# A one-core language-model tower: another order of TensorE's work ahead of the scan, dt products over all 128 rows, and the first dt*u products made inside the softplus

## What is computed

```python
xi, z = jnp.split(layernorm(x, gamma_in, beta_in) @ W_in, 2, axis=-1)
u = jax.nn.silu(depthwise_conv1d(xi, conv_w, conv_b))      # u; z gates the output later
proj = u @ x_proj_w                                         # 12 columns dt, 16 columns B, 16 columns C
dt = jax.nn.softplus(proj[..., :DT_RANK] @ dt_w + dt_b)     # DT_RANK = 12
A = -jnp.exp(A_log)
# per time step, 16 states per channel:
dA = jnp.exp(d_t[..., None] * A)
h = dA * h + (d_t * u_t)[..., None] * B_t[:, None, :]
y = jnp.einsum('bdn,bn->bd', h, C_t)
```

## Time and profile before

| | |
|---|---|
| device time, 3 runs | median 930.63 us (929.95, 930.63, 930.77) |
| the profiled execution | 930.0 us, of which the span from first to last instruction is 928.3 us |
| PE / DVE / ACT / POOL busy | 796.5 / 734.0 / 645.6 / 534.7 us |
| first scan of the loop starts | at 171.68 us |
| mean granted TensorE clock | 0.918 of full |

### The profile page before, as it was taken

How to read it: one execution, slowest core, us unless ns; L and a number is a source line. 1 busy time by engine, 2 the same in 40 slices (tenths; PEclk the granted TensorE clock), 3 DMA queues, 4 the chain that set the end, 5 groups by cost and what they waited for, 6 DMA issues and landing times.

```text
span 928.3 us, 16642 instructions
## 1 busy us (share of the span) xinstructions
PE 796.5 (86%) x6060; PEld 710.3 (77%) x6061; DVE 734.0 (79%) x873; ACT 645.6 (70%) x1258; POOL 534.7 (58%) x343
## 2 busy tenths in 40 slices
PE   0489796789998999999999999997986699999990
PEld 0223232789998999989999999996875699999990
DVE  3777489688999999998999999999849555555554
ACT  0264576999999999999999999993431444444431
POOL 6420000489997899987999889986000344444420
PEclk9989655899999999999999999999865799999996
DMA  4011200345476555664655746556480111111106
GB/s 86 2 68 43 32 4 26 120 119 152 139 164 200 159 144 176 141 200 125 149 171 146 215 121 157 194 125 196 116 275 1 39 42 42 42 45 44 43 26 212
DMA packets 46453, 104.43 MB, mean 112 GB/s; under 512 B 16448, under 2 KB 25176, under 8 KB 46392
## 3 DMA queue, kind: packets, MB, share of 16 engines
q1 hardware_dynamic: 35784, 74.67, 24.5%
q0 software_dynamic: 8352, 27.07, 14.7%
q10 hardware_dynamic: 2256, 1.87, 0.6%
HBM read 83.77 MB, written 19.82 MB: 112 GB/s over the span
## 4 chain that ended last, share of the span: by engine, by line
PE 52%; DVE 19%; ACT 14%; POOL 8%; issue 5%; DMA 2%; another core or an unknown queue 0%; DVEq 0%; ACTq 0%; POOLq 0%; SPq 0%
PE ps L1426 16%; DVE arena L840 8%; PE ps L1712 8%; PE ps L1535 8%; POOL arena L621 6%; PE ps L1695 6%; ACT arena L1261 5%; PE ps L1700 4%; ACT arena L1244 3%; PE ps L1494 3%; PE ps L1446 2%; PE ps L1476 2%; ACT arena L1247 2%; PE ps L1449 1%; DVE stats L667 1%
## 5 line engine op out<-in xcount | busy, mean ns | idle before, releaser
L621 POOL TENSOR_TENSOR arena<-arena 128x1024 f32<-128x1024 f32 x192 | 395.2, 2286 | 145.3 <-DVE arena L840 141.9
L840 DVE TENSOR_TENSOR_SCAN arena<-arena,ps 128x1024 f32<-128x1024 f32 x192 | 426.4, 2277 | 27.5 <-PE ps L1535 25.1
L1426 PE MATMUL ps<-ident,arena 128*128 128x128 f32 (+3 forms) x2622 | 349.5, 281 | 84.7 <-ACT arena L1128 35.0
L1426 PEld LDWEIGHTS ps<-ident,arena 128*128 128x128 f32 (+3 forms) x2622 | 300.9, 144 | 105.0 <-issue 50.6
L1261 ACT ACTIVATE arena<-arena,neg_a 128x510 f32<-128x510 f32 x384 | 241.1, 709 | 0.0
L625 POOL DMA_INDIRECT arena<-x_rows,arena x39 | 37.7, 968 | 160.5 <-DVE arena L1024 79.7
L1535 PE MATMUL ps<-arena,ln_in 128*128 128x128 f32 x768 | 102.8, 277 | 0.0
L1535 PE MATMUL ps<-arena 128*128 128x128 f32 x768 | 102.1, 276 | 0.0
L1535 PEld LDWEIGHTS ps<-arena,ln_in 128*128 128x128 f32 x768 | 94.7, 194 | 0.0
L1535 PEld LDWEIGHTS ps<-arena 128*128 128x128 f32 x768 | 93.9, 193 | 0.0
L1712 PE MATMUL ps<-arena,ln_in 128*128 x468 | 82.7, 327 | 0.8 <-DVE arena L1055 0.8
(11 more groups left out here) (216 smaller groups left out, 890.4 us busy)
## 6 DMA issues: line engine op xcount, KB each, us to landing
arena<-b_rows SPq DMA_DIRECT2D x64, 512.0 KB, 3.9
arena<-ws SPq DMA_DIRECT2D x16, 576.0 KB, 5.6
arena<-wf POOLq DMA_DIRECT2D x16, 576.0 KB, 7.7
arena<-hf POOLq DMA_DIRECT2D x16, 576.0 KB, 7.6
summed_first<-arena SPq DMA_DIRECT2D x8, 576.0 KB, 5.5
summed_second<-arena SPq DMA_DIRECT2D x8, 576.0 KB, 7.8
arena<-summed_second SPq DMA_DIRECT2D x8, 576.0 KB, 6.2
gates_dram<-arena SPq DMA_DIRECT2D x4, 768.0 KB, 3.5
```

What stands on the lines that cost most here:

```text
L621: g_.tensor_tensor(state[i % STATES], state[i % STATES], c_bc[u % C_BUFS], ALU.mult).then_inc(s_mul, 1)
L840: v.tensor_tensor_scan(o, a, x, 0.0, ALU.mult, ALU.add).then_inc(s_scan, 1)
L1426: return mm(o, src, ident[at:at + parts, at:at + parts], start=start, stop=True, is_transpose=True, skip_group_check=True)
```

## The change

Six edits, all ahead of the loop or in its first two units:

- PE's transposes of groups 2 and 3 are issued ahead: those of group 2 before the xi products of group 1, those of group 3 behind them. ACT's `keep_xn_t` calls move accordingly.
- ACT makes the `skip` diagonals before group 3's silus, and copies `lb[0]` out before the load of the table of Exp and Ln.
- The weights of the dt products are laid out as `dt_w_sb[128, 2, 384]`, zero outside a direction's 13 rows, and each product takes all 128 rows of `lb`. One more memset (128 x 768) stands in DVE's setup.
- PE issues `projections(g + 1)` between the dt products of direction 0 and of direction 1; ACT's `keep_lb(g + 1)` moves behind Ln of direction 0, `keep_bt(g)` behind Exp of direction 1.
- dt*u of group 0 has a tile for each direction and is made after rounds 4 and 5. Its transposes go through banks 0 and 1 one at a time (`FIRST_BANKS`): two among the last dt products, four after them, two after item 1 of the loop.
- ACT prepares unit 0 before the last rounds' DVE work is done: `scale_x(0)` waits for round 5 only, the edges of direction 0 and `exps(0)` for round 6; the edges of direction 1 go ahead of unit 1; four of the eight `keep_first_dtu_t` copies stand behind `exps(0)`.

```diff
@@ DVE
+            v.memset(dt_w_sb, 0.0)
...
+            def times_u(d):
+                v.tensor_tensor(dtu_b if d else dtu, dt_all[0][d], u_all[0], ALU.mult).then_inc(s_dtu, 1)
...
-                if n == 4:
-                    dve.wait_ge(s_dt, 1)
-                    times_u(0, 0)
-            dve.wait_ge(s_dt, 2)
-            times_u(0, 1)
+                if n in (4, 5):
+                    dve.wait_ge(s_dt, n - 3)
+                    times_u(n - 4)
             dve.wait_ge(s_dt, 2 * NG)
@@ ACT, softplus
-                    if d == 1 and g + 1 < NG:
-                        keep_lb(g + 1)
+                    if d == 1:
+                        keep_bt(g)
+                        if g == NG - 1:
+                            keep_first_dtu_t(1)
                     act.wait_ge(s_e, n + 1)
                     a.activation(dt, sp_e[n % SP], ACT.Ln, bias=1.0).then_inc(s_l, 1)
-                    if d == 0:
-                        keep_bt(g)
...
+                    if d == 0 and g + 1 < NG:
+                        keep_lb(g + 1)
+                    elif d == 0:
...
+                        keep_first_dtu_t(0)
@@ ACT, ahead of the loop
-            keep_first_dtu_t(0)
-            act.wait_ge(s_dt, 2 * NG)
...
+            keep_first_dtu_t(2)
+            keep_first_dtu_t(3)
             act.wait_ge(s_bt, NG)
+            act.wait_ge(s_dt, 2 * NG - 2)
             scale_x(0)
-            keep_first_dtu_t(1)
+            act.wait_ge(s_dt_ps, 2 * NG * DB)
+            act.wait_ge(s_dt, 2 * NG - 1)
...
+            edges(0)
             act.wait_ge(s_edge, 1)
             for u in range(NU):
                 g, r = divmod(u, UG)
+                if u == 1:
+                    act.wait_ge(s_dt, 2 * NG)
+                    edges(1)
+                    act.wait_ge(s_edge, 2)
                 exps(u)
+                if u == 0:
+                    for i in range(TG, 2 * TG):
+                        keep_first_dtu_t(i)
                 if u + 1 < NU:
                     scale_x(u + 1)
@@ PE, softplus
-                        mm(ps[:, DT_BANK + DB * d + blk, :], dt_w_sb[32 * d:32 * d + RANK + 1, P * blk:P * blk + P],
-                           lb[g % 2][32 * d:32 * d + RANK + 1, :], start=True, stop=True).then_inc(s_dt_ps, 1)
+                        mm(ps[:, DT_BANK + DB * d + blk, :], dt_w_sb[:, d, P * blk:P * blk + P],
+                           lb[g % 2], start=True, stop=True).then_inc(s_dt_ps, 1)
+                    if d == 0 and g + 1 < NG:
+                        projections(g + 1)
+                    if g == NG - 1:
+                        first_dtu_transposes(d)
...
-                if g + 1 < NG:
-                    projections(g + 1)
@@ PE, ahead of the loop and in it
+            def first_dtu_transposes(i):
+
+                d, t = divmod(i, TG)
+                pe.wait_ge(s_dtu, d + 1)
+                before_i = [j for j in range(i) if FIRST_BANKS[j] == FIRST_BANKS[i]]
+                if before_i:
+                    pe.wait_ge(s_dtu_t, before_i[-1] + 1)
...
-            pe.wait_ge(s_dtu_t, 2 * TG)
             LAG = 3
             for i in range(ITEMS + LAG):
+                if i < 2:
+
+                    pe.wait_ge(s_pl, 2 * NG - 1 + i)
                 if i < ITEMS:
                     x_blocks_of(i)
+                if i == 1:
+                    for n in range(TG + 2, 2 * TG):
+                        first_dtu_transposes(n)
+                if i == LAG:
+                    pe.wait_ge(s_dtu_t, 2 * TG)
```

More of the change, by code:

```diff
@@ L202, in build @@
         w_x = cut([DB, P])
-        dt_w_sb = cut([DI], parts=64)
+        dt_w_sb = cut([2, DI])
         after_params = used[0]
@@ L450, in _ @@
                 for blk in range(DB):
[L451 removed]
+                    loads.append((dt_w_sb[32 * d + RANK:32 * d + RANK + 1, d, P * blk:P * blk + P],
                                   chan[:, blk, CH_DTB + d:CH_DTB + d + 1].rearrange("p o -> o p")))
@@ L1153, in keep_u, with keep_lb @@
                 a.activation(u_all[g][:, blk, :], conv[g % 2][:, blk, :], ACT.Silu).then_inc(s_u, 1)
+            def keep_lb(g):
+                act.wait_ge(s_lb_ps, g + 1)
+                if g >= 2:
+                    act.wait_ge(s_c_st[g % 2], 32)
+                a.activation(lb[g % 2], ps[:, 0, :], ACT.Identity, scale=row_scale[:], bias=row_one[:]).then_inc(s_lb, 1)
             for blk in range(DB):
@@ L1159, in _ @@
             norm_in(3)
+            keep_xn_t(2)
             act.wait_ge(s_sz, DB)
@@ L1165, in _ @@
                 keep_u(0, blk)
-            keep_xn_t(2)
+            keep_xn_t(3)
             for blk in range(DB):
@@ L1172, in _ @@
             keep_z(2, 2, ACT.Silu)
-            keep_xn_t(3)
             keep_u(2, 1)
             keep_u(2, 2)
+            act.wait_ge(s_dm, 1)
+            act.wait_ge(s_ident, 1)
+            for blk in range(DB):
+                last = a.activation(skip[:, blk, :], ident[:], ACT.Copy, scale=d_merged[:, blk:blk + 1])
+            last.then_inc(s_skip, 1)
             keep_z(3, 0, ACT.Silu)
@@ L1192, in keep_bt @@
                 a.activation(bt[:, TG * g:TG * (g + 1), :], ps[:, 1, 0:TG * 2 * NS].rearrange("p (t n) -> p t n", t=TG), ACT.Copy).then_inc(s_bt, 1)
-            act.wait_ge(s_dm, 1)
-            act.wait_ge(s_ident, 1)
-            for blk in range(DB):
-                last = a.activation(skip[:, blk, :], ident[:], ACT.Copy, scale=d_merged[:, blk:blk + 1])
-            last.then_inc(s_skip, 1)
             a.preload_act_table_set("natural_log_exp_and_others")
-            act.wait_ge(s_bias_row, 1)
-            keep_lb(0)
             for g in range(NG):
@@ L1270, in scale_slow, with edges @@
                 last.then_inc(s_slow_w, 1)
-            act.wait_ge(s_res, 2)
-            act.wait_ge(s_xn, NG)
-            act.wait_ge(s_xn_ps, NG)
-            keep_first_dtu_t(0)
-            act.wait_ge(s_dt, 2 * NG)
-            for i in range(2):
-                act.wait_ge(s_c_st[i], 32 * NG // 2)
-            for d in range(2):
+            def edges(d):
                 for blk in range(DB):
@@ L1282, in _ @@
                     last = a.activation(edge, zeros[:], ACT.Copy)
-            last.then_inc(s_edge, 1)
+                last.then_inc(s_edge, 1)
+            keep_first_dtu_t(2)
+            keep_first_dtu_t(3)
             act.wait_ge(s_bt, NG)
+            act.wait_ge(s_dt, 2 * NG - 2)
             scale_x(0)
-            keep_first_dtu_t(1)
+            act.wait_ge(s_dt_ps, 2 * NG * DB)
+            act.wait_ge(s_dt, 2 * NG - 1)
+            for i in range(2):
+                act.wait_ge(s_c_st[i], 32 * NG // 2)
+            edges(0)
             act.wait_ge(s_edge, 1)
@@ L1486, in _, with dtu_transposes @@
             last.then_inc(s_rset, 1)
+            def dtu_transposes(src, t, at):
+                for blk in range(DB):
+                    c = at + P * blk
+                    last = transpose(ps[:, c // GT, c % GT:c % GT + P], src[:, blk, P * t:P * t + P], P)
+                last.then_inc(s_dtu_ps, 1)
+            def first_dtu_transposes(i):
[4 more added lines that the diff above has]
+                    pe.wait_ge(s_dtu_t, before_i[-1] + 1)
+                elif FIRST_BANKS[i] == 0:
+                    pe.wait_ge(s_lb, NG)
+                else:
+                    pe.wait_ge(s_bt, NG)
+                dtu_transposes(dtu_b if d else dtu, t, FIRST_BANKS[i] * GT)
             for g in range(NG):
@@ L1503, in _ @@
                 last.then_inc(s_bt_ps, 1)
-                if g + 1 < NG:
-                    projections(g + 1)
-            def dtu_transposes(g, d, t, at):
-                for blk in range(DB):
-                    c = at + P * blk
-                    last = transpose(ps[:, c // GT, c % GT:c % GT + P], dtu[:, blk, P * t:P * t + P], P)
-                last.then_inc(s_dtu_ps, 1)
-            for d in range(2):
-                pe.wait_ge(s_dtu, d + 1)
-                pe.wait_ge(s_pl, 2 * NG - 1 + d)
-                for t in range(TG):
-                    dtu_transposes(0, d, t, DT_BANK * GT + DB * GT * d + DI * t)
             def x_blocks_of(i):
```

41 lines of the change are left out of this document (19 added, 22 removed).

## The result

The changed kernel takes 907.03 us (median of 4 runs, 906.87 to 908.75), the kernel before 930.7 in the same comparison (929.95 to 931.22): a ratio of 0.975 with a 95% interval of 0.9734 to 0.9767, 23.7 us less. Forecast were 910.8 us and a range of 906 to 917. The profiled execution has a span of 905.1 us against 928.3, 23.2 less.

A forecast was written before the change was run, and what follows sets the result against it. DVE was taken as fullest in the softplus, yet waiting for ACT's Exp and Ln, and the loop as inheriting the start of `exps(1)`. Terms 5.8 + 2.25 + 2.7 + 5.5 + 3.5 = 19.8; 930.6 - 19.8 = 910.8 us, range 906 to 917.

The forecast's parts named there:

- front order: Front: transposes of groups 2 and 3 ahead save 4.1 us of PE's line, plus 1.7 by the clock; 5.8 us.
- skip, table load: Before the first dt products: skip diagonals (0.97) and table load (1.28) leave the chain; 2.25 us.
- first dt products: Ahead of DVE's first correction: three full-row products at clock 1.00 take 2.8 instead of 5.54 us; 2.7 us.
- softplus waits: Softplus: of DVE's 5.8 us of waits for Exp and Ln, 5.5 go; bounds 2 and 5.8.
- tail: From DVE's softplus end to `exps(1)`: 7.9 us instead of 11.4, a gain of 3.5; bounds 2.5 and 6.0.
- The clock part: Front: if PE's clock stays up, group 1's first xi product comes sooner; 1.7 us, bounds 0 and 1.9.
- the cover of 3 us: Softplus: the slack that hides the projections' new place, at no cost; without it each late us is DVE's.
- more comes: Tail: the clock is at 1.00 for round 7's products, 2.5 us more; 905 to 908; chance 0.09.
- Only part comes: Front clock part missing, half the softplus waits stay, tail copies wait on PE; 914 to 918; chance 0.20.
- PE bound: Softplus: clock stays 0.50, PE bounds, 923 us; 918 to 923 with part at 1.00; chance 0.055.
- slower: Loop: it gets PE at half clock, 6.6 us more a unit, losing from three such units on; chance 0.025.
- no effect: Loop: the start moves but something not tied to units, a DMA, holds the loop; chance 0.01.

The follow-up runs named there:

- e6: The kernel before with only the skip diagonals ahead of group 3's silus and `keep_lb(0)` ahead of the table load; 925.98 us.
- e3: The kernel before with only the front's order changed: transposes of groups 2 and 3 ahead, and the copies that follow them; 925.63 us.
- e7: The changed kernel with the first four dt*u transposes, their copies and `scale_x(0)` done before round 7 instead of after it; 905.52 us.
- e2: The kernel before with full-row dt products and nothing else; 926.07 us.
- e1: The changed kernel with the dt products at 13 rows each again, as before the change; 912.43 us.
- e4: The changed kernel with the old tail: dt*u of group 0, direction 1, at DVE's end, and unit 0 prepared behind it; 913.47 us.
- e5: The changed kernel with the next group's projections at the group's end again, and the copy into `lb` behind Exp of direction 1; 911.28 us.
- e8: The changed kernel with added products, results unused, in PE's holes of the softplus; 907.35 us.
- e9: The same kernel as e7, run again beside the changed kernel on one chip; 905.84 us.
- a1: The changed kernel as it is, measured again beside e8 and e9 on one chip; 908.32 us.

## Why the prediction was right, term by term

| term | forecast | in the two profiles |
|---|---|---|
| front order | 5.8 | 5.8 (8.04 to `keep_lb(0)`, less 2.28 of e6) |
| skip, table load | 2.25 | 2.28 (e6) |
| first dt products | 2.7 | 2.66 |
| softplus waits | 5.5 | 6.45 |
| tail | 3.5 | 4.56 |
| first convolution later | 0 | -0.27 |
| from `exps(1)` on | 0 | 1.70 |
| sum | 19.8 | 23.2 |

Measured were 907.03 us, 3.8 under the forecast of 910.8. Every mechanism that the sum names came, and its signs too: DVE without a hole from 94.26 to 146.96, a clock of 0.88 there, `exps(1)` at 153.66 (forecast 155.4). Two terms were sized too small (softplus by 0.95, tail by 1.06), and 1.70 came where I had put nothing. The time lies just below the sum's own part of the range (907.5 to 914).

*Front, chain and first products.* Forecast: `keep_lb(0)` near 88, measured 88.42; first correction at 94, measured 94.26. The clock part, put at 1.7 within 0 and 1.9, came with 1.3: the clock is 0.58 to 62.39 and 0.99 from there, and DVE waited 0.56 instead of 1.88 us. In e3 and e7 it stayed up and that wait went whole, so some 0.4 us of this term is the execution's and not the edit's. That the first products need both the full rows and the short hole is shown by e2 (full rows, hole left: the first correction came no sooner) and e1 (13 rows, hole of 0.37 us: 4.00 for three): closing the hole gave 1.5 of the 2.66 us there, the rows 1.16.

*Full rows against packed tiles.* The rival was that PE loses 3.3 us a group by giving up the overlap of two directions. The Trainium skill ("TensorE: Matmul & The Clock Gate", Part 3: Packing small matmuls) states that slicing lets tiles run concurrently; the trace agrees for the products themselves (e6: six of 13 rows in 5.79 us at a mean clock of 0.65; e2: six of 128 rows in 8.46 us at 0.64). It doesn't decide here: over the whole softplus e2 shows less busy time on PE with the full rows, by 12.9 us, and e1 what keeping the slices costs. Why the clock stays low under products of 13 rows, no run here shows.

*Softplus.* The mechanism was right, and the term was mis-sized by 0.95, above its own upper bound of 5.8. All 5.73 us of waits went. The bound left out that DVE's neighbouring instructions overlap when nothing stops them: in the changed kernel a correction starts 0.08 to 0.09 us before the instruction ahead of it has ended by the record, and DVE's busy time in the stretch fell from 52.83 to 52.11 with eight waits gone. A round without dt*u is then 6.12 us and not 6.2. e2 and e4 split the term by edit: full rows alone take 4.6 us off the stretch; with the front, `keep_lb` and the projections between the directions it is 6.45. e5, with the projections back at the group's end, keeps 0.98 us of waits; so their new place is worth 1.3 in the stretch, and the cover of 3 us that I had worked out for it held (e8: the stretch doesn't change when PE is faster).

*Tail.* The line was right, from `s_pl` of round 5 through round 7's products to `exps(1)`; the term was mis-sized by 1.06. I had put `exps(1)` at 7.9 us after DVE's end, and it came after 6.70. Of these 1.2 us, 0.9 are round 7's products, put at 0.50 and 5.3 us; they took 4.41, at 0.64. The remaining 0.3 is spread over ACT's pieces. Against it stand 0.14, since the tail before was 11.26 us and not 11.4. (The line's start, 1.8 + 1.7 + 12.4, is 15.9 and not 15.8 us ahead of DVE's end.) The forecast that DVE scans three items early and then waits held in kind (it waited 1.41 us, not 3). e5 and e8 show the two ends of the clock there: 5.49 and 2.84.

*The loop.* I had put it at nothing. From `exps(1)` to the end the profile of before has 753.2 us, that of after 751.5. The difference lies in one place, the first edge between groups. PE stands still for 1.99 us there in both kernels; then the windows of before and of after:

```profile
298.00:302.00 4.00, 2.01 (x15) 1.77 (x13) 4.00 (x6) 3.05 (x6) 1.52 (x2) 0.89 0.42 131
302.00:306.00 4.00, 4.00 (x27) 4.00 (x26) 2.91 (x3) 3.25 (x9) 3.42 (x3) 0.68 0.03 6
```

```profile
278.00:282.00 4.00, 3.02 (x27) 2.96 (x28) 4.00 (x3) 2.96 (x6) 2.82 (x2) 1.00 0.33 119
282.00:286.00 4.00, 4.00 (x38) 4.00 (x38) 4.00 (x3) 4.00 (x10) 3.58 (x3) 1.00 0.02 4
```

Where the clock falls the group takes 118.7 us, where it stays 117.1. In all twelve profiles it is 111.9 to 112.0 us from `exps(1)` to the first scan of the second group, and which of the three edges between groups loses the clock varies: two of them in before, e3, e4 and e6, one in the eight others, and not the same one in e7 and e9, which are one kernel. That speaks for chance. But from `exps(1)` to the end the five profiles with the old tail (before, e2, e3, e4, e6) take 753.2 to 754.0 us and the seven with the new tail 751.5 to 752.2, without overlap, and in e2 to e4 part of it lies behind the last scan (224 us to the end instead of 222 to 223). That speaks for a part of the new tail, by a way that I don't know. The timed runs show little of it: the median gain is larger than the gain in start by 1.1 us on average in e2, e3, e4 and e6 and by 0.7 in e1, e5, e7, e8, a1 and e9, where by the profiles it should be 1.9 larger than in the others. So whether these 1.70 us are chance or the change's stays open. The comparison of a1, 22.0 us less than before, against the first, 23.7, differs by as much.

The rivals: *more comes* (905 to 908, chance 0.09) names the time, but only half its reason: round 7's products were at 0.64, not 1.00, and e8, where they are at 1.00, gains only 0.6 us of start by it. Without the 1.70 us of the loop the time would lie inside the sum's own part of the range, so that the number fell to this rival is partly luck. *Only part comes*, *PE bound*, *slower* and *no effect* didn't occur.

## What to carry to other kernels

A product with few rows can be the dearer one even where two of them overlap: here 13-row products left TensorE busy and its clock mostly at half, and the same products over all rows, padded with zeros, made PE's busy time in the softplus 29% shorter (e2). That is one shape (f32, 13 rows, 512 columns), so try it on yours. Price a hole of PE with the slow work behind it. And follow a tail to the operation that bounds the loop (`exps(1)` here), since a faster PE in it gave 0.6 us of start (e8), while moving unit 0's work into ACT's wait of 2.6 us gave 3.2 us of start (e7, e9) and 2.5 of time (e9 against a1).
